# Scores of the first element straight from T, and a run of zero matmuls ahead of the first loads, in a fused attention kernel

## The reference, cut to what matters

```python
def reference(x, Wq, bq, Wk, bk, Wv, bv, Wo, bo):
    g = _gn(x)                                # 8 groups over M, eps 1e-5
    Q = einsum('oc,bscm->bsom', Wq, g) + bq   # 256 outputs o
    K = einsum('oc,bscm->bsom', Wk, g) + bk
    V = einsum('oc,bscm->bsom', Wv, g) + bv
    QK = Q.transpose(b,m,o,s) @ K.transpose(b,m,s,o)   # (8, 16, 256, 256)
    A = softmax(QK, axis=-1)
    out = einsum('bmcC,bmsC->bsCm', A, Vp)    # Vp is V as (b, m, s, o)
    return x + einsum('oc,bscm->bsom', Wo, out) + bo
```

## Time and profile before

| what | value |
|---|---|
| median of 3 runs | 199.22 us (196.81 to 209.14) |
| profiled execution | 199.71 us, of which the span from first to last instruction is 197.9 us |
| PE busy | 165.7 us (84%) |
| DVE busy | 130.8 us (66%) |
| ACT busy | 128.8 us (65%) |
| POOL busy | 99.5 us (50%) |
| mean granted PE clock | 0.911 of full speed |

### The profile page before, as it was taken

How to read it: one execution, slowest core, us unless ns; L and a number is a source line. 1 busy time by engine, 2 the same in 40 slices (tenths; PEclk the granted TensorE clock), 3 DMA queues, 4 the chain that set the end, 5 groups by cost and what they waited for, 6 DMA issues and landing times. The chain is left out here.

```text
span 197.9 us, 5954 instructions
## 1 busy us (share of the span) xinstructions
PE 165.7 (84%) x2208; PEld 89.7 (45%) x2208; DVE 130.8 (66%) x291; ACT 128.8 (65%) x529; POOL 99.5 (50%) x122
## 2 busy tenths in 40 slices
PE   0697096999897899999999999989897898799753
PEld 0263035555454545564545455535454453464330
DVE  0355429748886788778777878788778766654241
ACT  0200005957798688788868887988798998874401
POOL 3353656404897299497558755963642303214000
PEclk9999758569999999999999999999999999955975
DMA  5900585893299169639933972588079502200202
GB/s 192 365 6 0 108 196 96 199 239 146 31 199 252 66 131 205 210 62 197 260 137 58 208 206 81 76 196 264 12 128 215 201 0 109 103 6 0 106 5 106
DMA packets 9626, 26.61 MB, mean 134 GB/s; under 512 B 2459, under 2 KB 3326, under 8 KB 9598
## 3 DMA queue, kind: packets, MB, share of 16 engines
q1 hardware_dynamic: 8224, 25.57, 50.1%
q10 hardware_dynamic: 1374, 0.67, 1.3%
HBM read 9.06 MB, written 4.19 MB: 67 GB/s over the span
## 5 line engine op out<-in xcount | busy, mean ns | idle before, releaser
L772 ACT ACTIVATE e_sb<-s_bank,negmax 128x256 f32<-128x256 f32 x256 | 117.6, 495 | 49.6 <-DVE negmax L584 27.9
L584 DVE TENSOR_REDUCE negmax<-s_bank 128x2 f32<-128x512 f32 x128 | 87.1, 686 | 24.4 <-PE s_bank L404 23.1
L404 PE MATMUL s_bank<-stack,wq_st 99*128 99x256 f32 x256 | 63.2, 341 | 3.7 <-ACT e_sb L772 2.5
L404 PEld LDWEIGHTS s_bank<-stack,wq_st 99*128 99x128 f32 x256 | 39.8, 201 | 41.0 <-issue 40.7
L772 ACT ACTIVATION_READ_ACCUMULATOR e_sb<-s_bank,negmax 128x1 f32 x256 | 58.1, 227 | 0.0
L414 PE MATMUL acc<-e_sb,recip 128*32 128x256 f32 x512 | 43.4, 412 | 9.4 <-DVE recip L590 8.9
L815 POOL TENSOR_TENSOR xc<-xs,nm 128x512 f32<-128x512 f32 x15 | 15.9, 1082 | 20.1 <-DVE nm L543 20.1
L866 POOL TENSOR_TENSOR t_parts<-t_sb,t_parts 128x1280 fp32r<-128x1280 f32 x7 | 20.4, 2908 | 4.3 <-DVE t_parts L579 3.8
L565 DVE SCALAR_TENSOR_TENSOR t_sb<-bk_sb,ssum,bz 128x256 f32<-128x256 f32 x28 | 12.9, 465 | 12.4 <-PE bz L382 10.4
L879 POOL TENSOR_TENSOR ws<-wo_sb,aT 128x1024 f32<-128x1024 f32 x7 | 13.4, 1912 | 14.2 <-DVE aT L600 14.2
L414 PEld LDWEIGHTS acc<-e_sb,recip 128*32 128x32 f32 x512 | 10.7, 111 | 20.8 <-DVE recip L590 13.8
(11 more groups left out here) (72 smaller groups left out, 128.8 us busy)
## 6 DMA issues: line engine op xcount, KB each, us to landing
stack<-t_parts SPq DMA_DIRECT2D x32, 256.0 KB, 4.9
xs<-x_rows SPq DMA_DIRECT2D x8, 512.0 KB, 5.7
stack<-t_parts SPq DMA_DIRECT2D x32, 128.0 KB, 4.8
xT<-x_cols SPq DMA_DIRECT2D x8, 512.0 KB, 6.0
y_cols<-yb SPq DMA_DIRECT2D x7, 512.0 KB, 4.1
y_cols<-yb SPq DMA_DIRECT2D x2, 256.0 KB, 2.0
stack<-t_parts SPq DMA_DIRECT2D x8, 32.0 KB
k_sb<-consts ACTq DMA_DIRECT2D x1, 235.5 KB, 4.5
```

What stands on the lines that cost most here:

```text
L404: mm = nc.tensor.matmul(s_bank[p % NS][:, CH * h:CH * h + CH], wq_st[:, P * h:P * h + P], stack[:, side, p % Q, p // Q, :], start=True, st ...
L584: nc.vector.tensor_reduce(negmax[:, p % NS, :], s_bank[p % NS][:, :].rearrange("p (h n) -> p h n", h=HC), op=ALU.max, axis=AX.X, negate=Tr ...
L772: last = nc.scalar.activation(e_sb[:, p % NE, h, :], s_bank[p % NS][:, CH * h:CH * h + CH], ACT.Exp, bias=negmax[:, p % NS, h:h + 1], accu ...
```

## The change

Four things are done.

1. PE starts with five matmuls of 128 x 256 zeros into a score bank that is still free. They wait only for a memset of the zeros.
2. Element 0 has no stack any more. Its scores are made from `t_sb` itself in plain f32, over the 32 rows of position q, and the bias is added in the same bank by a second matmul, over 12 rows, of split copies of bq and of the bias row. The halves are paired, (p, 1) with (p + 1, 0), so that two matmuls of different row groups and different banks stand next to each other. The first score of element 0 then needs only the first quarter of T. New data is loaded and prepared for this: `wq_rep` and `bq_rep`, 128 KB each, and `bq_rows`, a 128 x 1024 multiplication on POOL.
3. What element 1 and the second half of T of element 0 need is moved from the straight code into the slots of element 0: `ANCHOR[1]` is 1, its ten stack transfers wait for a high part in slot 6. `split_wq` goes to slot 9. The low part of element 1 stands on POOL behind `diagonal(2)`, which was behind it before.
4. The steps of elements 2, 3 and 4 move: T of element 2 from slot 7 to slot 13, of element 3 from 22 to 24, of element 4 from 36 to 37, and their statistics come closer to it. `gnorm` and `ssum` have two buffers. SP loads the columns of element 0 right after the first four loads of rows.

The core of the diff:

```diff
-ANCHOR = {2: 7, 3: 22, 4: 36, **{j: M * (j - 2) + 3 for j in range(5, B)}}
+ANCHOR = {0: 0, 1: 1, 2: 13, 3: 24, 4: 37, **{j: M * (j - 2) + 3 for j in range(5, B)}}
+HI_FIRST, SPLIT_WQ = 6, 9
...
+            def tb_product_first():
+                pe.wait_ge(sblk_done, 1)
+                nc.tensor.matmul(by[:, 0:CH], sblk_first[:, :, :, :].rearrange("p q k t -> p (q k t)"), wk_sb[:, :],
+                                 start=True, stop=True).then_inc(tb_mm, 1)
+
+            def score_first(halves):
+                for p, h in halves:
+                    t, q = p // Q, p % Q
+                    pe.wait_ge(t_read, t + 1)
+                    after(pe, exped, p - NS + 1)
+                    rows = slice(C * q, C * q + C)
+                    nc.tensor.matmul(s_bank[p % NS][:, CH * h:CH * h + CH], wq_sb[rows, P * h:P * h + P],
+                                     t_sb[rows, 0, t, :], start=True, stop=False)
+                for p, h in halves:
+                    t, q = p // Q, p % Q
+                    rows = slice(C * q, C * q + NP * T)
+                    mm = nc.tensor.matmul(s_bank[p % NS][:, CH * h:CH * h + CH], bq_rows[rows, t, P * h:P * h + P],
+                                          tb_st[rows, :], start=False, stop=True)
+                    if h == HC - 1:
+                        mm.then_inc(scores, 1)
+
             def score(b, p):
+                if b == 0:
+                    score_first([(p, 1), (p + 1, 0)] if p + 1 < M else [(p, 1)])
+                    return
...
+            pe.wait_ge(set_zeros, 1)
+            for _ in range(5):
+                nc.tensor.matmul(s_bank[0][:, 0:CH], t_sb[:, 0, T, 0:P], t_sb[:, 0, T, :], start=True, stop=True)
             pe.wait_ge(k_loaded, 16)
             sum_rows(0)
             mean(0)
             sum_rows(1)
             gram_of(0)
             mean(1)
             variance(0)
-            sum_rows(2)
-            pe.wait_ge(w_loaded, 16 * 7)
+            pe.wait_ge(w_loaded, 16 * 8)
             t_product(0, 0, t01_mm, bz)
-            tb_product(0)
-            t_product(0, 2, t23_mm, t23_bank(0))
+            tb_product_first()
             gram_of(1)
-            mean(2)
+            pe.wait_ge(bq_done, 1)
+            pe.wait_ge(tb_split, 2)
+            score_first([(0, 0)])
+            score(0, 0)
+            score(0, 1)
             variance(1)
-            t_product(1, 0, t01_mm, bz)
-            tb_product(1)
-            t_product(1, 2, t23_mm, t23_bank(1))
-            pe.wait_ge(set_dve, 2)
-            for p in range(AHEAD):
-                score(0, p)
+            score(0, 2)
...
+                    if slot == HI_FIRST:
+                        high_part(1)
+                    if slot == SPLIT_WQ:
+                        split_wq()
...
+            def read_tb_first():
+                dve.wait_ge(tb_mm, 1)
+                nc.vector.scalar_tensor_tensor(tb_rows[:, :], bk_sb[:, :], rows_all[:, :], by[:, 0:CH],
+                                               ALU.mult, ALU.add).then_inc(tb_done, 1)
+                dve.wait_ge(tb_done, 1)
+                nc.vector.tensor_copy(tb_hi[:, :], tb_rows[:, :]).then_inc(tb_split, 1)
+                dve.wait_ge(tb_split, 1)
+                nc.vector.scalar_tensor_tensor(tb_st[:, :], tb_hi[:, :].bitcast(f32), k_sb[:, TLO:TLO + 1], tb_rows[:, :],
+                                               ALU.mult, ALU.add).then_inc(tb_split, 1)
...
-            dve.wait_ge(set_pool, 1)
+            centre_chunk(1)
+            dve.wait_ge(w_loaded, 16 * 8)
+            dve.wait_ge(set_zeros, 3)
             read_t(0, 0)
+            read_tb_first()
+            read_gram(1)
             read_t(0, 1)
-            read_tb(0)
-            read_t(0, 2)
-            read_t(0, 3)
-            high_part(0)
-            read_gram(1)
-            low_part_first()
             sum_diagonal(1)
+            maximum(0, 0)
             read_variance(1)
-            read_mean(2)
-            read_t(1, 0)
-            read_t(1, 1)
-            read_tb(1)
-            read_t(1, 2)
-            read_t(1, 3)
-            high_part(1)
-            for p in range(LEAD):
-                maximum(0, p)
+            maximum(0, 1)
...
             centre_rows(0, chunks=(1,))
             column_means(0)
-            centre_rows(1)
+            pool.wait_ge(bq_split, 2)
+            nc.gpsimd.tensor_tensor(bq_rows[:, :, :], bq_st[:, None, :].bitcast(f32).to_broadcast([P, T, CH]),
+                                    k_sb[:, PICKT:PICKT + T, None].to_broadcast([P, T, CH]), ALU.mult
+                                    ).then_inc(bq_done, 1)
+            centre_rows(1, chunks=(1,))
             power(0)
             scaled_sums(0)
...
             column_means(2)
+            diagonal(2)
             low_part(1)
-            diagonal(2)
```

More of the change, by code:

```diff
@@ L280, in bias @@
                     sp.dma_start(dst.bitcast(f32), src.bitcast(f32)).then_inc(bias_stacked[side], 16)
-                if j == 0:
-                    high(0)
-                    bias(0)
-                    sp.wait_ge(parts_done, 1)
-                    low(0)
-                    bias(1)
-                    for q in range(1, Q):
-                        high(q)
-                        low(q)
-                else:
-                    for q in range(Q):
-                        high(q)
-                    bias(0)
-                    sp.wait_ge(parts_done, j + 1)
-                    bias(1)
-                    for q in range(Q):
-                        low(q)
+                for q in range(Q):
+                    high(q)
+                bias(0)
+                sp.wait_ge(parts_done, j)
+                bias(1)
+                for q in range(Q):
+                    low(q)
             def store(j):
@@ L381, in t_product @@
                         rows = slice(C * q, C * q + C)
-                        mm = nc.tensor.matmul(dst[rows, CH * i:CH * i + CH], gnorm[rows, first + i, :],
+                        mm = nc.tensor.matmul(dst[rows, CH * i:CH * i + CH], gnorm[rows, j % 2, first + i, :],
                                               wk_sb[rows, :], start=True, stop=True)
@@ L686, in split_wq, with split_bq @@
                                                ).then_inc(set_dve, 1)
+            def split_bq():
+                dve.wait_ge(bq_loaded, 16)
+                nc.vector.tensor_copy(bq_hi[:, :], bq_sb[:, :]).then_inc(bq_split, 1)
+                dve.wait_ge(bq_split, 1)
+                nc.vector.scalar_tensor_tensor(bq_st[:, :], bq_hi[:, :].bitcast(f32), k_sb[:, BLO:BLO + 1], bq_sb[:, :],
+                                               ALU.mult, ALU.add).then_inc(bq_split, 1)
             def diagonal_first():
@@ L900, in _ @@
             column_means(1)
-            pool.wait_ge(w_loaded, 16 * 7)
-            for h in range(HC):
-                last = nc.gpsimd.tensor_scalar(wobv[:, h], wo_sb[:, h, :], bv_sb[:, h:h + 1], 0.0, ALU.mult, ALU.add)
-            last.then_inc(set_pool, 1)
             diagonal(1)
@@ L908, in _ @@
             scaled_sums(1)
+            pool.wait_ge(w_loaded, 16 * 8)
+            for h in range(HC):
+                last = nc.gpsimd.tensor_scalar(wobv[:, h], wo_sb[:, h, :], bv_sb[:, h:h + 1], 0.0, ALU.mult, ALU.add)
+            last.then_inc(set_pool, 1)
             centre_rows(2)
             column_means(2)
+            diagonal(2)
             low_part(1)
-            diagonal(2)
             power(2)
```

149 lines of the change are left out of this document (93 added, 56 removed).

## The result

The changed kernel takes 218.12 us (median of 4 runs, 217.06 to 219.65), against 200.3 us (196.81 to 209.14) for the kernel before on the same chip: ratio 1.102, 95% interval 1.086 to 1.118. It is slower by 10%. The forecast was 192.8 us, with 0.07 for slower. The profiled execution took 217.87 us, with a span of 216.1 us and a mean granted clock of 0.813 (before 0.911). Single executions of one kernel differ by how long PE is at half clock (of 52 of the kernel before, seven took over 208 us), and the ratios compare the fast ones.

What follows compares the result with a forecast made beforehand. PE was taken to bound element 0 behind a start of small chained steps. 18.4 + 1.3 + 28.3 + 0.7 = 48.7 us puts its mark 6.9 us earlier, so 199.71 less 6.9 is 192.8 us, range 188 to 198.5.

Steps and rivals of the forecast that it cites:

- first mark: `read_acc` of element 0, forecast at 48.7 us against 55.58 before, 6.9 us earlier.
- first exponential: End of the start's chain of small steps on ACT, forecast at 18.4 us against 31.99 before.
- start of element 0's PE work behind it: PE starts the summed work of element 0 about 1.3 us behind the first exponential.
- work on PE that is no pair: Element 0's stack scores, column sums, T products and small matmuls, priced at full clock: 17.1 us.
- 12.5 pairs: Element 0's new scores on PE, 0.90 us per pair between bounds of 0.68 and 1.42: 11.3 us.
- waits, the read and the rest: End of element 0: the read behind the last sum and small waits, 0.7 us.
- Slower: half clock in element 0: Rival: PE at half clock in element 0 loses 0.5 per us; 196.9 us or beyond 203; chance 0.10.
- rival of serial pairs: Element 0's scores: a pair's two f32 matmuls run one after the other, 6.5 us more, 199.3 us; chance 0.13.
- gain of 1.0: At the start: the five zero matmuls' effect on PE's clock, taken as -1.0 us between +0.4 and -3.0.
- late stack: Rival: element 1's stack comes late, PE stands at slot 13 for 2 to 4 us, 195 to 197 us; chance 0.12.

Runs made afterwards that it cites:

- e6_zeros_in_gaps: Kernel before with zero matmuls at the start (5), ahead of the variance of element 1 (5) and behind it (3): 198.08 us.
- e11_all_rows_gaps: Changed kernel with element 0's f32 scores over all 128 rows, zero weights outside the tile's 32, and seven more zero matmuls in holes before the first score: 208.56 us.
- e9_gaps_filled: Changed kernel with seven more zero matmuls over 128 rows in four holes of PE before the first score: 209.81 us.
- e4_full_filler: Changed kernel with one more f32 matmul of zeros over 128 rows in each pair of element 0's scores: 232.99 us.
- e10_gaps_and_full_rows: Changed kernel with seven more zero matmuls in holes before the first score and one 128-row reduced-type zero matmul per pair: 228.99 us, ratio 1.148.
- m4_data_and_holes: Kernel before, preceded by pairs like the new scores: real x without holes, then zeros and real x with a hole after every third pair; total time not given.
- m1_ladder: Kernel before, preceded by hole-free f32 zero matmuls: 128-row stretches alternating with 32-row ones, single, two and four side by side; total time not given.
- m2_pairs_ladder: Kernel before, preceded by hole-free zero pairs of 32-row f32 matmuls, alone first, then with 12-row or 32-row bias matmuls, parted by 128-row stretches; total time not given.

## Why the prediction was wrong, step by step

The forecast had the first mark at 48.7; it came at 71.53, 22.8 later. By its terms:

| term | forecast | measured | off by |
|---|---|---|---|
| first exponential | 18.4 | 21.24 | +2.8 |
| start of element 0's PE work behind it | +1.3 | +1.2 | -0.1 |
| work on PE that is no pair | 17.1 | 29.6, by the distance of starts of each | +12.5 |
| 12.5 pairs | 11.3 | 12.5 x 1.36 = 17.0 | +5.7 |
| waits, the read and the rest | 0.7 | 2.5, with 1.28 at the variance of element 2 | +1.8 |

- **The failed step is the last clause of the rival "Slower: half clock in element 0": "PE is more densely fed than before, and a dense PE came back to full clock at about 44 us after some 11 us."** PE was denser, and stayed at half clock for 61 us. The recovery, at 43.2 us, came among the stack's scores over 99 rows, and the change takes those out of element 0. The argument took "busy" from one form of matmul to another, and one spell of some 11 us for the rule: work of the old form itself took 14 us behind the last pair of after (56.1 to 70.4), and 20 in `e6_zeros_in_gaps`. The rival's own arithmetic (each us at half clock loses 0.5, 21 us of it for 2%) was sound. Its chance of 0.10 was too low, as far as one outcome can say. TensorE: Matmul & The Clock Gate of the Trainium skill, section What's actually happening, says that activity releases the throttle. The windows of after, 5.00 of 5 us busy at 0.50, say that busy time alone did not; here the measurement decides.
- **Two terms of the sum were mis-sized by it.** Of the 5.7 us on pairs, the clock makes 12.5 x (1.36 - 0.66) = 8.7; at full clock the price was 0.66, so my 0.90 was 3.0 too much. The true price lies just below the lower bound (0.68) of my range. The rival of serial pairs did not occur (0.35 us for both f32 matmuls). Whether 0.107 us of exposed weight load are in the 0.66 no run shows: the two bias matmuls take 0.31 of it, against 0.24 for two streams of 0.12. The other 12.5 us are clock alone.
- **First exponential, +2.8.** The zeros did what was taken for likely at 5.6 (0.64 for the row sums), but the clock was lost again in the holes, at 9.0. I had booked a gain of 1.0 beyond it; the T product took the old 1.93. Some 0.8 us more went where the sum had DVE's reads back to back. PE works on the bias row of T first (L416, 1.22 us at half clock), and DVE waits for it:
```profile
16.58 0.48 DVE L765 SCALAR_TENSOR_TENSOR tb_rows<-bk_sb,rows_all,by 128x256 f32<-128x256 f32 x1 [0.48 <-PE by L416]
```
The first scores, at half clock, took the last 0.9: 2.5 us from 18.01 to the first maximum at 20.52, against 1.6.
- **The late stack did not occur.** The seven elements behind kept their length but for 1.8 us. At half clock the transfers had more time than the forecast gave them, so this is a weak test; but in `e11_all_rows_gaps`, near full clock, PE did not wait for the stack of element 1 either.
- **Waits in element 0.** I set them at near nothing. After has 1.9 us of them, and `e11_all_rows_gaps`, mostly at full clock, 3.3 (1.39, 1.46 and 0.46 for `recip`), which the sum did not have.

The terms add up to 71.5. By them, after at full clock would have its mark at about 71.5 - 12.5 - 8.7 = 50.3, an estimate: close to the 48.7 of the forecast, before the longer waits that `e11_all_rows_gaps` uncovered. No traced run kept full clock with the pairs over 32 rows, so this is argued and not shown.

**What stays open.** That half clock in element 0 is the loss is shown by the prices. Why the clock fell and stayed down is shown only in part. The form of the scores matters (`e9_gaps_filled` against `e11_all_rows_gaps`, and the ladders), and so do the holes of the start. But 128-row fillers did not hold the clock in `e4_full_filler` beyond 47.6 us, nor in `e10_gaps_and_full_rows` at all, though `e11_all_rows_gaps`, without a 32-row score, held it; and `e6_zeros_in_gaps` was at half clock for 20 us without such a score. Whether holes as small as those of `m4_data_and_holes`, or the rate of matmuls, are what loses it in the kernel itself is open too: a version with the pairs and no hole in element 0 was not made.

## What to carry over

Before moving work to a matmul over fewer rows, ask what it does to the clock of all else on PE: price the whole stretch at half clock too, and give that case real weight, since PE busy at 100% was no protection here, with the new form (after) or the old (`e6_zeros_in_gaps`). When a granted clock recovers in a trace, note which form of matmul ran then, whether the change keeps it, and do not take one recovery for the rule. Zeros on an idle PE are cheap: ahead of the first loads they gave 1.2% with the old order, and seven more in the holes of the start gave 8.3 us with the new one.

## What the hardware showed that was not expected

- PE stayed at half clock for 61 us (9.0 to 70.4), in most of the last 50 busy for 5.00 of 5 us (after). Single 32-row matmuls without a hole fell from full to half clock after 4.3 us (13.02 to 17.35, `m1_ladder`), while 128-row matmuls on zeros raised it after 4.8 (39.84 to 44.65).
- Two 32-row matmuls side by side neither lose the clock without holes nor raise it in 25 us; with a hole of 0.20 us after every third pair, and so at about half the rate, they lost it after 12.5 us on zeros and 6.5 on real data (`m4_data_and_holes`). The same page of the Trainium skill, section A second HAM failure mode: psum-queue depth-cycling, tells of short idle times between groups of matmuls that cost the clock; that trace agrees as to the fall, with 0.20 us; it shows no way back under the pairs.
- The clock's record starts at 1.00 although rows run at half speed: in `m2_pairs_ladder` a pair took 0.84 us where the side-by-side form at full clock takes 0.43. Durations are the safer witness there.
